# A weight product of 1160 columns, split 392, 384 and 384 instead of 512, 320 and 328

## The chip, the cores and the metric

The kernel runs on one core of a Trainium2 chip. The metric is the device time of one execution in microseconds. TensorE (PE) multiplies, VectorE (DVE), ScalarE (ACT) and GpSimd (POOL) work elementwise, SyncE (SP) issues most of the DMAs. A product takes a stationary operand of 128 x 128, loaded before it (PEld), and streams the columns of the moving operand through it into a PSUM bank of 512 float32 columns.

## The reference, cut to what matters

Two adapter layers over 4096 tokens (64 x 64) of width 1024:

```
x = x + A0[id] (B0[id] x)                     # low rank 16, one adapter of 64 for each sequence
base   = x W^T                                # 1024 x 1024
logits = x Wr^T + 5.0 * onehot(lang)          # 8 experts
gates  = softmax of the two largest logits
h      = x A^T                                # 8 experts x rank 16 = 128 columns
x = x + base + 2 * sum over e of gates_e (h_e B_e^T)
```

## The kernel before

The tokens are cut into T = 32 tiles of 128. Everything that the second layer multiplies x with stands in one matrix of 128 + 8 + 1024 = 1160 columns: A (ER = 128 columns), the router Wr (8 more, so NH = 136 columns ahead of W), and W transposed, with the identity added so that the product also gives x + base. It is kept in two halves, w_hi and w_lo, each with C = 8 chunks of 128 rows. A chunk takes PITCH = 1184 words, of which the last 24 are padding; the first chunk starts at word 28 of a line of 32.

Each tile needs x1_hi w_hi + x1_hi w_lo + x1_lo w_hi over 8 chunks, so K3 = 24 products for each group of columns. The 1160 columns are split into three PARTS, one for each of the PSUM banks O[0], O[1] and O[2]: columns 0 to 511, 512 to 831 and 832 to 1159. Part 0 holds h and the logits and 376 of the output's columns. make_part (line 602) issues the products of a part; first_part (578) does so for tile 0 in pieces between the transposes of the weight's nine blocks, and PART_BLOCKS says for which blocks each part waits.

TensorE's order for a tile n from 1 on (lines 689 to 705), written out by hand:

```
make_bx for 0 or 2 later tiles (line 501)
make_part(n, 0)              # 24 products; then the logits are there (h_psum)
add_l0(n + 1)  (n + 1 < 7)   # or
make_x1(n + 2) (n + 2 >= 7)  # lines 523 to 530; waits for bx_step, a_lo_ready, x_put
make_part(n, 1); turn_gated(n); make_part(n, 2) up to product 12
add_lora(0); add_lora(1)     # line 622, three products each, wait for gt_ready
make_part(n, 2) from product 12; add_lora(2)
```

From n = 5 on make_bx is done for two tiles together ahead of an odd n. Its result goes through ScalarE (swap and pair copies, lines 751 and 758) and VectorE (lines 965 to 980) to bx_t. VectorE then runs choose_experts and weigh_experts (998 to 1025), turns x1 of the next tile (924), makes the two halves of the turned gates (gated_t_part: gt_hi at 1031, gt_lo), x1_lo, and for later tiles b_raw (935), a_raw (945) and xt (917). a_raw goes to ScalarE for the high half of a_t (a_hi_part, 731) and to GpSimd for the low half (a_lo_part, 417), which tells a_lo_ready; between its a_lo_parts GpSimd gathers later adapters by indirect DMA. ScalarE copies the three banks to out_sb (out_part, 805), and SyncE stores a tile's row block when all three are there. The last tile is stored in three pieces (376, 320 and 328 columns).

add_lora streams lb_hi and lb_lo, whose 1024 columns start at word 4 of a line, so the slices for parts 1 and 2 (from columns 376 and 696) start at word 28.

Of the kernel before, what the change touches and what calls it, by code (L numbers as in the profile page):

```python
# [12 lines left out]
P = 128  # L13
LANG_BIAS = 5.0
BANK = 512
# [4 lines left out]
def two_adapter_layers(nc, x, adapter_ids, lang_ids, l0_A, l0_B, l1_W, l1_Wr, l1_A, l1_B, out):  # L20
    NB, S, D = x.shape
    NAD, R, _ = l0_B.shape
    E = l1_Wr.shape[0]
    T = NB * S // P
# [11 lines left out]
    PITCH = (NW + LINE - 1) // LINE * LINE  # L36
    REST = (NW - BANK) // 2 // LINE * LINE
    PARTS = [(0, BANK), (BANK, BANK + REST), (BANK + REST, NW)]
    NP = len(PARTS)
# [20 lines left out]
    with ExitStack() as ctx:  # L60
# [217 lines left out]
        UNIT_BANK_X0 = {12: 0, 13: 1}  # L278
        PART_BLOCKS = ((0, 1, 2, 3), (3, 4, 5, 6), (6, 7, 8))

# [8 lines left out]
        def weight_cols(b):  # L289
            return slice(0, ER) if b == 0 else slice(NH + (b - 1) * P, NH + b * P)  # L290

# [29 lines left out]
        def _(sp):  # L321
# [42 lines left out]
            for n in range(T):  # L364
# [6 lines left out]
                if n < T - 1:  # L371
                    for k in range(NP):
                        sp.wait_ge(out_ready[k], n + 1)
                    sp.dma_start(out_rows[n * P:(n + 1) * P, :], out_sb[:, n % 2, :]).then_inc(out_stored[n % 2], 16)
            for k, (lo, hi) in enumerate(PARTS):
                lo = max(lo - NH, 0)
                sp.wait_ge(out_ready[k], T)
                sp.dma_start(out_rows[(T - 1) * P:T * P, lo:hi - NH],
                             out_sb[:, (T - 1) % 2, lo:hi - NH]).then_inc(last_stored, 16)
            sp.wait_ge(out_stored[T % 2], 16 * (T // 2))  # L380
# [102 lines left out]
        def _(pe):  # L483
# [134 lines left out]
            def add_lora(part):  # L618
                lo, hi = PARTS[part]
                skip = NH if part == 0 else 0  # L620
                for k, (gt, lb) in enumerate(((gt_hi, lb_hi), (gt_hi, lb_lo), (gt_lo, lb_hi))):
                    mm = pe.matmul(O[part][:, skip:hi - lo], gt[:, :], lb[:, lo + skip - NH:hi - NH],  # L622
                                   start=False, stop=(k == 2), skip_group_check=True)
                mm.then_inc(o_psum, 1)
# [83 lines left out]
        def _(act):  # L708
# [90 lines left out]
            def out_part(n, part):  # L799
                lo, hi = PARTS[part]  # L800
                skip = NH if part == 0 else 0
                if part == 0 and n >= 2:
                    act.wait_ge(out_stored[n % 2], 16 * (n // 2))
                act.wait_ge(o_psum, NP * n + part + 1)
                nc.scalar.copy(out_sb[:, n % 2, lo + skip - NH:hi - NH],  # L805
                               O[part][:, skip:hi - lo]).then_inc(out_ready[part], 1)
# [402 lines left out]
```

## Time and profile before

| what | value |
|---|---|
| median of 3 runs | 525.18 us (523.86 to 525.43) |
| span of the profiled execution | 523.2 us |
| what lies around the span, by the median | 2.0 us |
| PE busy | 510.4 us, 98% |
| PEld / DVE / ACT / POOL busy | 89% / 73% / 46% / 33% |
| granted TensorE clock, mean | 0.993 |
| HBM traffic | 189 GB/s over the span |

The profiled execution is listed by its span, the time from the first to the last instruction; no time of its own is given beside it. A PE share of 98% doesn't say that TensorE is at its peak: neighbouring products overlap, and their ends are modelled.

### The profile page before, as it was taken

To read this page: it belongs to the slowest core of one execution; us is meant where nothing else is said; L and a number is where in the kernel's file an instruction comes from. 1 tells how busy PE (TensorE), PEld (TensorE's weight loads), DVE (VectorE), ACT (ScalarE), POOL (GpSimd) and SP (SyncE) were. 2 spreads that over 40 slices of the span, in tenths; PEclk is the share of its full clock that TensorE was granted. 3 is DMA by queue.
4 is the path that set the end of the run, shared out by engine and by line. 5 is a ranking of instruction groups with operands and counts; after the bars stand their busy time and mean duration, and the time that the engine had idled before them with its cause. 6 is when DMAs were issued, how large, how long until landed. Compare 5 with 4: busy or idle time off the path is not lost.

```text
span 523.2 us, 9432 instructions
## 1 busy us (share of the span) xinstructions
PE 510.4 (98%) x3350; PEld 465.7 (89%) x3350; DVE 383.9 (73%) x882; ACT 240.6 (46%) x543; POOL 171.1 (33%) x159
## 2 busy tenths in 40 slices
PE   7699999999899999999999999999999999999997
PEld 6588999889899899999989899998989999898997
DVE  5779686758879686977968697796969779693441
ACT  4655433545354544445454445554544545543221
POOL 5442325634314434142443414143441414321000
PEclk9799999999999999999999999999999999999999
DMA  8942455637757768477785857878576767633301
GB/s 330 322 114 82 130 134 170 205 111 233 231 185 231 229 153 260 169 219 238 245 239 152 248 184 222 247 222 245 155 225 207 243 225 213 202 105 98 122 40 41
DMA packets 52467, 99.76 MB, mean 191 GB/s; under 512 B 6716, under 2 KB 35260, under 8 KB 52420
## 3 DMA queue, kind: packets, MB, share of 16 engines
q1 hardware_dynamic: 45744, 78.14, 48.7%
q0 software_dynamic: 6656, 20.98, 12.7%
q8 instruction: 27, 0.44, 0.3%
q14 instruction: 20, 0.16, 0.1%
q10 hardware_dynamic: 20, 0.03, 0.0%
HBM read 69.24 MB, written 29.88 MB: 189 GB/s over the span
## 4 chain that ended last, share of the span: by engine, by line
PE 87%; DVE 7%; issue 2%; ACT 1%; DMA 1%; POOL 1%; another core or an unknown queue 0%; DVEq 0%; POOLq 0%
PE o_bank L609 69%; PE o_bank L622 8%; PE b_bank L501 2%; PE o_bank L598 2%; PE x_bank L529 2%; DMA a_in<-in_L_cond_A_dram,a_run 1%; DVE a_raw L945 1%; PE x_bank L519 1%; DVE x_lo L882 1%; PE b_bank L486 1%; DVE xt L917 1%; PE x_bank L486 1%; ACT bx_pair L758 1%; DVE w_in L924 0%; DVE b_raw L935 0%
## 5 line engine op out<-in xcount | busy, mean ns | idle before, releaser
L609 PE MATMUL o_bank<-w_hi,x_hi 128*128 128x512 f32 (+1 forms) x744 | 255.6, 344 | 0.0
L609 PE MATMUL o_bank<-w_lo,x_hi 128*128 128x512 f32 (+1 forms) x744 | 251.1, 337 | 0.0
L609 PE MATMUL o_bank<-w_hi,x_lo 128*128 128x512 f32 (+1 forms) x744 | 250.9, 337 | 0.0
L417 POOL TENSOR_TENSOR a_t<-a_raw,a_t 64x1024 fp32r<-64x1024 f32 x30 | 72.3, 2411 | 248.9 <-ACT a_t L731 178.3
L609 PEld LDWEIGHTS o_bank<-w_hi,x_hi 128*128 128x128 f32 x744 | 139.8, 188 | 13.5 <-issue 3.2
L609 PEld LDWEIGHTS o_bank<-w_lo,x_hi 128*128 128x128 f32 x744 | 139.9, 188 | 10.1
L609 PEld LDWEIGHTS o_bank<-w_hi,x_lo 128*128 128x128 f32 x744 | 139.7, 188 | 10.2
L945 DVE STREAM_TRANSPOSE a_raw<-a_in 128x1024 f32<-128x1024 f32 x32 | 65.3, 2044 | 2.8 <-DMA a_in<-in_L_cond_A_dram,a_run 2.8
L388 POOL DMA_INDIRECT a_in<-in_L_cond_A_dram,a_run x64 | 61.0, 952 | 19.3 <-issue 19.0
L731 ACT CAST a_t<-a_raw 128x1024 fp32r<-128x1024 f32 x32 | 33.6, 1050 | 70.0 <-DVE a_raw L945 69.9
L805 ACT COPY out_sb<-o_bank 128x376 f32<-128x376 f32 (+2 forms) x96 | 39.5, 443 | 52.6 <-PE o_bank L622 52.6
L924 DVE STREAM_TRANSPOSE w_in<-w_in 128x512 f32<-128x512 f32 x50 | 58.7, 1196 | 0.1
L917 DVE STREAM_TRANSPOSE xt<-x_in 128x512 f32<-128x512 f32 x50 | 56.1, 1158 | 0.0
L770 ACT CAST x_hi<-w_in 128x512 fp32r<-128x512 f32 x50 | 31.1, 621 | 43.2 <-DVE w_in L924 43.2
L758 ACT COPY bx_pair<-bx_half 32x128 f32<-32x128 f32 x120 | 35.6, 297 | 22.7 <-DVE bx_half L965 11.2
L394 POOL DMA_INDIRECT b_in<-in_L_cond_B_dram,b_run x32 | 30.8, 964 | 23.4 <-DVE a_t L882 8.6
L973 DVE TENSOR_TENSOR bx_all<-bx_half,bx_pair 128x128 f32<-128x128 f32 x30 | 8.8, 292 | 39.0 <-ACT bx_pair L758 37.6
L882 DVE TENSOR_TENSOR x_lo<-w_in,x_hi 128x512 fp32r<-128x512 f32 x50 | 35.0, 722 | 2.0 <-ACT x_hi L770 2.0
L622 PE MATMUL o_bank<-lb_hi,gt_hi 128*128 128x376 f32 (+2 forms) x96 | 30.6, 319 | 0.6 <-DVE gt_lo L882 0.6
L622 PE MATMUL o_bank<-lb_lo,gt_hi 128*128 128x376 f32 (+2 forms) x96 | 30.5, 318 | 0.0
L622 PE MATMUL o_bank<-lb_hi,gt_lo 128*128 128x376 f32 (+2 forms) x96 | 30.4, 317 | 0.0
L965 DVE TENSOR_TENSOR bx_half<-b_bank,bx_swap 128x128 f32<-128x128 f32 x30 | 8.6, 288 | 29.6 <-ACT bx_swap L751 27.7
(111 smaller groups left out, 504.3 us busy)
## 6 DMA issues: line engine op xcount, KB each, us to landing
out_dram<-out_sb SPq DMA_DIRECT2D x31, 512.0 KB
x_in<-in_x_dram SPq DMA_DIRECT2D x120, 128.0 KB
w_in<-in_x_dram SPq DMA_DIRECT2D x25, 512.0 KB
x_dram<-w_in SPq DMA_DIRECT2D x25, 512.0 KB, 4.4
w_in<-x_dram SPq DMA_DIRECT2D x100, 128.0 KB
w_in<-in_L_cond_W_dram SPq DMA_DIRECT2D x6, 512.0 KB, 13.3
x_in<-in_x_dram SPq DMA_DIRECT2D x2, 512.0 KB
out_sb<-in_L_cond_W_dram SPq DMA_DIRECT2D x2, 512.0 KB, 15.1
```

Of the source, the lines that this page charges most:

```text
L388: pool.indirect_dma_start(a_in[:, m % 2, b, :], None, l0_A_runs, bass.IndirectOffsetOnAxis(ap=a_run[:, m * BPT + b:m * BPT + b + 1], axis= ...
L417: nc.gpsimd.tensor_tensor(lower, a_raw[Q:P, m % 2, :], lower.bitcast(F32), ALU.subtract)\
L609: mm = pe.matmul(O[part][:, 0:hi - lo], xs[:, n % 2, c, :], w[:, c, lo:hi], start=(k == 0), stop=(k == K3 - 1), skip_group_check=True)
L622: mm = pe.matmul(O[part][:, skip:hi - lo], gt[:, :], lb[:, lo + skip - NH:hi - NH], start=False, stop=(k == 2), skip_group_check=True)
L731: nc.scalar.copy(a_t[:, m % 2, :], a_raw[:, m % 2, :]).then_inc(a_hi_ready, 1)
L758: nc.scalar.copy(bx_pair[q * SQ:(q + 1) * SQ, :], bx_half[o * SQ:(o + 1) * SQ, :]).then_inc(pair_ready, 1)
L770: nc.scalar.copy(x1_hi[:, m % 2, chunks(h), :], src).then_inc(x1_hi_ready, 1)
L805: nc.scalar.copy(out_sb[:, n % 2, lo + skip - NH:hi - NH], O[part][:, skip:hi - lo]).then_inc(out_ready[part], 1)
L882: return nc.vector.tensor_tensor(dst, raw, hi.bitcast(F32), ALU.subtract)
L917: nc.vector.transpose(xt[:, m % 2, chunks(h), :].rearrange("p k (g i) -> p k g i", i=SQ), src[:, chunks(h), :, :]).then_inc(t1_ready, 1)
L924: nc.vector.transpose(x1_t[:, chunks(h), :].rearrange("p k (g i) -> p k g i", i=SQ), src[:, chunks(h), :, :]).then_inc(x1t_ready, 1)
L945: nc.vector.transpose(cols, a_in[:, m % 2, :, :].rearrange("p b (f r) -> p f b r", r=R)).then_inc(aT_ready, 1)
```

## The change

The parts become columns 0 to 391, 392 to 775 and 776 to 1159 of the matrix, 392, 384 and 384 columns. The 24 words of padding move from the end of each chunk to between parts 0 and 1, so that part 1 starts at word 416 and part 2 at word 800 of a chunk, each again at word 28 of a line. The blocks of W that make up the parts become 0 to 2, 3 to 5 and 6 to 8, whole blocks each. The output's columns are split 256, 384 and 384 in place of 376, 320 and 328 (OUTS), in add_lora, in out_part and in the three stores of the last tile. The slices of lb_hi and lb_lo start at columns 0, 256 and 640, word 4 of a line each. The numbers of products, copies and DMAs stay as they were, and so does their order.

```
-    REST = (NW - BANK) // 2 // LINE * LINE
-    PARTS = [(0, BANK), (BANK, BANK + REST), (BANK + REST, NW)]
+    FIRST = 2 * P
+    HALF = (D - FIRST) // 2
+    GAP = PITCH - NW
+    PARTS = [(0, NH + FIRST), (NH + FIRST + GAP, PITCH - HALF), (PITCH - HALF, PITCH)]
+    OUTS = [(0, FIRST), (FIRST, FIRST + HALF), (FIRST + HALF, D)]
...
-        PART_BLOCKS = ((0, 1, 2, 3), (3, 4, 5, 6), (6, 7, 8))
+        PART_BLOCKS = ((0, 1, 2), (3, 4, 5), (6, 7, 8))
...
         def weight_cols(b):
-            return slice(0, ER) if b == 0 else slice(NH + (b - 1) * P, NH + b * P)
+            if b == 0:
+                return slice(0, ER)
+            at = NH + (b - 1) * P + (GAP if (b - 1) * P >= FIRST else 0)
+            return slice(at, at + P)
...
-            for k, (lo, hi) in enumerate(PARTS):
-                lo = max(lo - NH, 0)
+            for k, (lo, hi) in enumerate(OUTS):
...
-                    mm = pe.matmul(O[part][:, skip:hi - lo], gt[:, :], lb[:, lo + skip - NH:hi - NH],
+                    mm = pe.matmul(O[part][:, skip:hi - lo], gt[:, :], lb[:, OUTS[part][0]:OUTS[part][1]],
...
-                nc.scalar.copy(out_sb[:, n % 2, lo + skip - NH:hi - NH],
+                nc.scalar.copy(out_sb[:, n % 2, OUTS[part][0]:OUTS[part][1]],
```

## Rows read from the trace of the kernel before

**Rows 1.** The page: its span, TensorE's share, the chain that ended last.

```profile
span 523.2 us, 9432 instructions
...
PE 510.4 (98%) x3350; PEld 465.7 (89%) x3350; DVE 383.9 (73%) x882; ACT 240.6 (46%) x543; POOL 171.1 (33%) x159
...
PE 87%; DVE 7%; issue 2%; ACT 1%; DMA 1%; POOL 1%; another core or an unknown queue 0%; DVEq 0%; POOLq 0%
```

**Rows 2.** Chain in order of time, tiles 11 and 12: start us, us, what.

```profile
204.19 5.68 PE o_bank L609 x24
...
213.84 0.11 PE b_bank L486
...
218.96 5.50 PE o_bank L609 x24
...
224.92 3.51 PE o_bank L609 x24
...
228.54 1.81 PE o_bank L609 x12
...
231.31 1.81 PE o_bank L609 x12
...
234.58 0.42 PE o_bank L609
```

**Rows 3.** Timelines of tiles 11 and 12, by engine: start us, us, instruction.

```profile
204.25 0.54 ACT L751 COPY bx_swap<-b_bank 64x128 f32<-64x128 f32 x2 [0.61 <-PE b_bank L501]
...
210.56 0.15 DVE L998 SCALAR_TENSOR_TENSOR logit<-is_lang,o_bank 128x8 f32<-128x8 f32 x1
...
212.68 1.20 DVE L924 STREAM_TRANSPOSE w_in<-w_in 128x512 f32<-128x512 f32 x1
213.99 0.29 DVE L1031 CAST gt_hi<-b_bank 128x128 fp32r<-128x128 f32 x1
...
217.67 2.04 DVE L945 STREAM_TRANSPOSE a_raw<-a_in 128x1024 f32<-128x1024 f32 x1
...
219.75 1.05 ACT L731 CAST a_t<-a_raw 128x1024 fp32r<-128x1024 f32 x1 [2.58 <-DVE a_raw L945]
...
220.88 2.41 POOL L417 TENSOR_TENSOR a_t<-a_raw,a_t 64x1024 fp32r<-64x1024 f32 x1 [12.67 <-ACT a_t L731]
...
224.29 0.63 PE L529 MATMUL x_bank<-a_t,bx_t 128*128 128x512 f32 x2
```

**Rows 4.** Line 528, the wait of TensorE's sequencer in tile 12: ns, start us.

```profile
L528 PEldq EVENT_SEMAPHORE  x1: 3130/3130/3130, 220.2 to 220.2; - x1
```

**Rows 5.** Timeline, tile 10: first products of add_lora(0) and add_lora(1).

```profile
199.80 0.33 PE L622 MATMUL o_bank<-lb_hi,gt_hi 128*128 128x376 f32 x1
...
200.32 0.31 PE L622 MATMUL o_bank<-lb_hi,gt_hi 128*128 128x320 f32 x1
```

**Rows 6.** Timeline, tile 4: a product that waited for VectorE, and the next.

```profile
105.34 0.29 DVE L882 TENSOR_TENSOR gt_lo<-b_bank,gt_hi 128x128 fp32r<-128x128 f32 x1
...
105.69 0.44 PE L622 MATMUL o_bank<-lb_hi,gt_hi 128*128 128x376 f32 x1 [0.62 <-DVE gt_lo L882]
105.97 0.33 PE L622 MATMUL o_bank<-lb_lo,gt_hi 128*128 128x376 f32 x1
```

**Rows 7.** Timeline, tile 0: the first four products of part 0.

```profile
23.17 2.05 PE L598 MATMUL o_bank<-w_hi,x_hi 128*128 128x512 f32 x4
```

**Rows 8.** Timeline ahead of tile 7: VectorE, GpSimd and the wait of make_bx.

```profile
136.60 3.49 DVE L882 TENSOR_TENSOR x_lo<-w_in,x_hi 128x512 fp32r<-128x512 f32 x2
136.80 2.74 POOL L417 TENSOR_TENSOR a_t<-a_raw,a_t 64x1024 fp32r<-64x1024 f32 x1 [4.37 <-DMA a_in<-in_L_cond_A_dram,a_run]
...
142.74 0.64 PE L501 MATMUL b_bank<-xt,b_raw 128*32 128x128 f32 x16 [1.34 <-DVE b_raw L935]
```

**Rows 9.** Groups of ScalarE by form, 200 to 500 us: busy us, mean ns, idle before.

```profile
L805 ACT COPY out_sb<-o_bank 128x376 f32<-128x376 f32 x20 | 9.4, 472 | 13.3 <-PE o_bank L622 13.3
L805 ACT COPY out_sb<-o_bank 128x328 f32<-128x328 f32 x20 | 8.6, 428 | 20.1 <-PE o_bank L622 20.1
```

More of the change, by code:

```diff
@@ L374, in _ @@
                     sp.dma_start(out_rows[n * P:(n + 1) * P, :], out_sb[:, n % 2, :]).then_inc(out_stored[n % 2], 16)
-            for k, (lo, hi) in enumerate(PARTS):
-                lo = max(lo - NH, 0)
+            for k, (lo, hi) in enumerate(OUTS):
                 sp.wait_ge(out_ready[k], T)
-                sp.dma_start(out_rows[(T - 1) * P:T * P, lo:hi - NH],
-                             out_sb[:, (T - 1) % 2, lo:hi - NH]).then_inc(last_stored, 16)
+                sp.dma_start(out_rows[(T - 1) * P:T * P, lo:hi],
+                             out_sb[:, (T - 1) % 2, lo:hi]).then_inc(last_stored, 16)
             sp.wait_ge(out_stored[T % 2], 16 * (T // 2))
```

## The prediction

> **What bounds the kernel now.** I read the page first. TensorE is busy for 98% of the span and carries 87% of the chain that ended last, almost all of it in the weight product of line 609 [rows 1]. So TensorE sets the pace, and the question is what the new split does to its 2,232 products and to what it waits for. A matmul's own mean duration doesn't help here, since neighbours overlap; the chain in order of time gives the stretches without overlap [rows 2]. There, two token tiles (n = 11 and 12; tiles alternate like this to the end, a pair with two make_bx in front of its odd tile) take 234.58 - 204.19 = 30.39 us with no gap on TensorE. Then I looked for what reaches TensorE just in time, because a new split changes when each wait is reached: the timeline of the other engines over the same pair [rows 3] and the wait of TensorE's sequencer [rows 4].
>
> **The products themselves.** In the even tile part 0 (24 products of 512 columns) takes 5.50 us, 229.2 ns each; part 1 (24 of 320) 3.51 us, 146.3 ns each; part 2 (24 of 328) 1.81 + 1.81 = 3.62 us, 150.8 ns each [rows 2]. That is nearly a straight line: (229.2 - 146.3) / 192 = 0.432 ns a column, and 146.3 + 8 x 0.432 = 149.8 for 328. On that line 392 columns take 229.2 - 120 x 0.432 = 177.4 ns and 384 take 174.0 ns. Part 0 becomes 4.26 us, parts 1 and 2 4.18 us each, 12.61 us a tile against 12.63. Next to nothing is gained or lost: the number of products (72 a tile) and of columns (1160) is the same. The new parts still begin at word 28 of a 32-word line, since the 24 padding words stand after the column 392, so alignment of w_hi and w_lo gives no reason to leave the line.
>
> Bounds, since 384 and 392 columns don't occur in the trace: what a product takes beyond its columns at 2.4 GHz is 146.3 - 133.3 = 13.0 ns for 320 and 229.2 - 213.3 = 15.9 ns for 512. With 13.0 for all, three products take 522.2 ns, with 15.9 for all 530.9 ns, against 526.3 now. Over 24 x 31 = 744 such triples that is -3.1 us and +3.4 us if TensorE sets the pace everywhere. I take the line, because 328 lies within 1 ns of it.
>
> As a rule: the Trainium skill (TensorE: Matmul & The Clock Gate, section Back-to-back issue gap) gives N / 2.4 + 2.5 ns for a warm product. The trace disagrees in size: 229.2 ns for 512 columns where the rule has 215.8. The rule too is linear, so by it three products take 490.8 ns before and after, and part 0 gets shorter by 24 x 50.0 = 1.20 us where the rows give 1.24; the stall worked out below would be 0.16 us by it instead of 0.20.
>
> **The nine products of add_lora.** Three of 376 columns take 200.32 - 199.80 = 0.52 us, 173.3 ns each [rows 5]; on the line it would be 170.5, so they lie 3 ns above it. Its operand lb_hi starts at word 4 of a line, where parts 1 and 2 start at word 28 today; in the new split all three start at word 4. By the line, 3 x 118.6 + 6 x 174.0 = 1.40 us, as today (3 x (173.3 + 146.3 + 150.8) = 1.41 us); with 3 ns more on the six that move, 1.42 us. I take +0.02 us a tile; the bounds are 0 and 0.04.
>
> **What comes earlier, and the wait it reaches.** Part 0 is now 5.50 - 4.26 = 1.24 us shorter and parts 1 and 2 are 0.67 and 0.56 us longer. Everything that TensorE asks for behind part 0 is asked for 1.24 us earlier. That is the step that I expect to decide. In an even tile make_x1(n + 2) stands right behind part 0 and needs the lower half of a_t from GpSimd (a_lo_ready). The chain to it starts in the odd tile before, with make_bx on TensorE, and runs through ScalarE and VectorE: swap at 204.25 (the wait before it ended by TensorE), the bx chain, the gate, the turned x1, x_lo, a_raw at 217.67, a_t high half on ScalarE at 219.75, low half on GpSimd from 220.88 to 223.29 [rows 3]. TensorE reaches make_x1 at 224.29: 1.00 us to spare. The sequencer is there much sooner and stands in that wait from 220.2 for 3.13 us [rows 4], hidden now by products already queued.
>
> This chain doesn't get shorter with part 0. VectorE comes to choose_experts at 210.56, after two bx chains, when part 0 (204.19 + 5.68 = 209.87) is done already; from there to a_raw it works almost without a gap. One piece moves: gt_hi at 213.99 waits for the turned gates, since VectorE was free at 212.68 + 1.20 = 213.88 and starts a next instruction some 0.06 us before the end of the last. In the new split parts 0 and 1 of the odd tile together are 0.57 us shorter, the turned gates are there before, and gt_hi starts at 213.82. So the chain ends 0.17 us earlier, at 223.12.
>
> TensorE gets to make_x1 at 224.29 - 1.24 + 0.02 = 223.07. A late hand-over has a price of its own: where gt_lo ended at 105.63, the product behind it started at 105.69 and the next 0.28 us later instead of 0.17 [rows 6]; the first weight load is then not hidden. I take 0.05 + 0.10 us: make_x1 effectively at 223.27, a stall of **0.20 us**. The pair is then 30.59 us instead of 30.39. It can't be made up behind: from make_x1 to the next pair TensorE has its own work, and the next chain starts with its make_bx. The stall falls in the even tiles n = 8 to 28 (n + 2 up to 30), 11 times: 11 x 0.20 = **+2.2 us**. Bounds: no cost at the hand-over and the 0.17 gained, 0.05 us each, +0.6 us; nothing gained at gt_hi and the full hand-over, 0.37 us each, +4.1 us.
>
> The other waits behind part 0 hold: in the odd tile make_x1 needs only the first of the two bx chains, which are both done by about 210.6, so that the first is through well before 208.5; the gates are done when VectorE goes on to its next transpose at 212.68, and TensorE turns them at 213.84 - 0.57 = 213.3 [rows 2, 3]. What queues behind the stalled make_x1 is only TensorE's own part 1; ScalarE's copy of x1 and the logits of VectorE wait less than now.
>
> **First tiles.** Tile 0 runs its first four products of part 0 at the lower clock level: 2.05 us for four [rows 7], 0.43 us apart, which is 512 columns at 1.2 GHz. Fewer columns there save about 0.4 us, and it is given back, because parts 1 and 2 are longer and the chain of make_bx(2) is released as before. In tiles 1 to 6 TensorE already waits here and there on VectorE (1.3 us on b_raw in front of tile 7 [rows 8], 0.6 us on gt_lo in tile 4 [rows 6]); VectorE and ScalarE, which don't get faster, set the end of that stretch. A shift of TensorE alone is swallowed by the 1.3 us wait. I take 0, bounds -0.7 and +0.6 us. PART_BLOCKS asks for fewer blocks; those waits don't end late now, so nothing.
>
> **End.** The last copy has 384 columns instead of 328: by the copies' means (472 - 428) / 48 = 0.9 ns a column [rows 9], +0.05 us. The copies of parts 1 and 2 in the loop are longer and that of part 0 shorter; ScalarE idles there.
>
> **Sum.** 523.2 + 2.2 + 0.05, and 0 for the rest, is a span of about 525.4 us. The median of the runs is 525.18, 2.0 us above the span of the profiled execution (the span runs from the first instruction to the last). So 527.4 us.
>
> **Rivals.**
> (A) The forecast: GpSimd's a_lo decides the even tiles. 526.8 to 529.4 us. Chance 0.55.
> (B) The change does nothing: the line holds and the chain ends some 0.2 us earlier than I think, for instance because ScalarE's longer idle time lets a copy in before. All stalls are 0.05 or less: 525.2 + 0.5 = 525.7, between 524 and 526.5. For it: the margin that decides is 0.2 us of a 19 us chain. Chance 0.22.
> (C) Faster: the logits come 1.2 us earlier in each tile, and the 1.3 us wait on b_raw goes away. Two x_lo of VectorE shortly before it take 3.49 us, most of it beside GpSimd's a_t (136.80 to 139.54) [rows 8]. If both ended before 136.80, b_raw would come some 2 us sooner. The two take 1.3 us where GpSimd is idle, so they would have to start by 135.5, 1.1 us earlier; VectorE waits there for the turned gates and gains some 0.3 us. That is against it. With the 0.6 us of tile 4 too and no stall later: 525.2 - 1.3 - 0.6 = 523.3 us. Chance 0.12.
> (D) The products cost the upper bound: 530.9 - 526.3 = 4.6 ns a triple. TensorE's own pair is 30.39 + 48 x 0.0046 + 0.04 = 30.65 us, and since 0.16 us of that lies ahead of make_x1, the stall shrinks to 0.04: 30.69 us, 15 pairs, 525.2 + 4.5 = 529.7 us. Chance 0.11.
>
> **Numbers.** The likeliest is A, 527.4 (its own range 526.8 to 529.4). The range 524.3 to 530.0 takes in B nearly whole and D, and leaves out C and the tails. 0.3% is 1.6 us and about what a measurement tells from no change: slower by more than that, over 526.8, is A and D less the low edge of A, 0.60; within is most of B and a bit of A and C, 0.28; faster 0.12.
>
> **What the profile would show.** Products of 392 and 384 columns starting 177 and 174 ns after one another; part 0 at 4.26 us in the chain; in even tiles a gap of some 0.2 us on TensorE in front of line 529, released by GpSimd's a_t, and the chain in order of time going through GpSimd, ScalarE and VectorE 11 times; pairs of 30.6 us. The forecast is wrong if a pair takes 30.4 us with no gap (B), if make_bx in front of tile 7 starts 1 us earlier than at 142.74 (C), or if 384 columns take 176 ns (D).

## The result, and the profile after

The changed kernel takes **530.22 us** (median of 4 runs, 529.4 to 531.2) against 524.86 us (523.86 to 525.43) for the kernel before beside it: a ratio of 1.0107, 95% interval 1.0083 to 1.0131. The forecast was 527.4 us with a range up to 530.0. The sign was right, and about half of the loss was not foreseen.

The page of the changed kernel (its span, the busy shares, the chain that ended last), to be held against [rows 1]:

```profile
span 528.8 us, 9430 instructions
...
PE 516.1 (98%) x3350; PEld 498.9 (94%) x3350; DVE 380.4 (72%) x882; ACT 241.7 (46%) x543; POOL 171.2 (32%) x159
...
PE 88%; DVE 4%; issue 3%; ACT 1%; DMA 1%; another core or an unknown queue 1%; POOL 1%; DVEq 0%; POOLq 0%
```

The span grew by 5.6 us, and "another core or an unknown queue" now has 1% of the chain. There is one core only, so that entry is a wait whose releaser the profile doesn't show.

Next the chain of the changed kernel in order of time over tiles 11 and 12 (start us, us, what), the stretch of [rows 2]:

```profile
207.97 4.49 PE o_bank L614 x24
212.46 0.46 PE x_bank L534 x2
212.93 4.20 PE o_bank L614 x24
...
222.81 4.25 PE o_bank L614 x24
227.06 0.59 PE x_bank L534 x2
227.64 4.19 PE o_bank L614 x24
...
237.52 1.01 PE b_bank L506 x32
238.53 1.63 PE o_bank L614 x8
```

Part 0 takes 4.25 us (forecast 4.26) and part 1 4.19 (4.18). make_x1 (line 534 now) takes 0.59 us in the even tile and 0.46 in the odd one: there is the forecast stall, smaller than I made it. The pair, 207.97 to 238.53, is 30.56 us; over the ten pairs of tiles 8 to 27 the mean is 30.58 us against 30.39 before.

The waits of the changed kernel (engine, line, waited for: us in total, times, longest):

```profile
ACT bx_swap L756 <- remote: 3.7, 1, 3.7
PEld x_bank L534 <- DVE bx_t L985: 2.6, 1, 2.6
PEld x_bank L534 <- issue: 2.4, 11, 0.4
```

The third row, put down to "issue", is the stall of the ten even tiles from 10 to 28, and one wait more in tile 5; tile 8, behind the long tile 7, has no stall in this execution. The first two rows belong together and happen once, ahead of and in tile 7. As in the kernel before, make_bx for tiles 9 and 10 runs ahead of tile 7, and make_x1(9), for tile 9, stands in tile 7. The timeline of the changed kernel there (start, us, engine, line, what, in brackets the idle time before and its releaser):

```profile
141.86 0.96 POOL L399 DMA_INDIRECT b_in<-in_L_cond_B_dram,b_run  x1 [0.77 <-POOL a_t L422]
141.97 1.08 PE L506 MATMUL b_bank<-xt,b_raw 128*32 128x128 f32 x32
143.13 0.95 POOL L393 DMA_INDIRECT a_in<-in_L_cond_A_dram,a_run  x1 [0.30 <-issue]
144.38 0.95 POOL L393 DMA_INDIRECT a_in<-in_L_cond_A_dram,a_run  x1 [0.30 <-issue]
146.21 0.54 ACT L756 COPY bx_swap<-b_bank 64x128 f32<-64x128 f32 x2 [3.66 <-remote]
149.79 1.22 PE L534 MATMUL x_bank<-a_t,bx_t 128*128 128x512 f32 x2 [2.25 <-DVE bx_t L985]
```

make_bx ended at 141.97 + 1.08 = 143.05, and ScalarE, which waits for both of its results, began the swap at 146.21: 3.16 us late. TensorE then stood 2.25 us in front of make_x1(9). Two stretches of the changed kernel, around that stand and over a steady pair (us, then busy us of PE, PEld, DVE, ACT and POOL with their instructions, granted clock, DMA share, GB/s):

```profile
141.00:156.30 15.30, 13.05 (x92) 12.06 (x91) 5.90 (x25) 6.54 (x19) 2.95 (x4) 0.89 0.72 215
208.00:238.50 30.50, 30.50 (x201) 29.64 (x201) 23.84 (x54) 14.86 (x34) 9.01 (x8) 1.00 0.67 202
```

From 149.5 us, in the last 0.3 us of that stand, to 152.9 us the granted clock was 0.5 (1.2 GHz), and the part 1 that fell into it took 5.12 us in the chain instead of 4.20. Tile 7 took 18.68 us from its part 0 to the next, against 14.70 before.

So the 5.6 us are: **+4.0 us** in tile 7, **+2.0 us** from tile 8 to the end, and -0.3 us from the start to tile 7. Of these only the second was forecast.

### The profile page after: what moved, and what is told of

Same layout as the page of the kernel before. It is cut to its first block, busy times and chain, and to the rows that moved or that the text cites. A ratio compares the mean times of both kernels' runs of the same rounds, so it can differ in the third digit from the quotient of the medians.

```text
span 528.8 us, 9430 instructions
## 1 busy us (share of the span) xinstructions
PE 516.1 (98%) x3350; PEld 498.9 (94%) x3350; DVE 380.4 (72%) x882; ACT 241.7 (46%) x543; POOL 171.2 (32%) x159
## 4 chain that ended last, share of the span: by engine, by line
PE 88%; DVE 4%; issue 3%; ACT 1%; DMA 1%; another core or an unknown queue 1%; POOL 1%; DVEq 0%; POOLq 0%
PE o_bank L614 69%; PE o_bank L627 8%; PE o_bank L603 3%; PE x_bank L534 3%; PE b_bank L506 2%; DMA a_in<-in_L_cond_A_dram,a_run 1%; PE x_bank L524 1%; PE x_bank L491 1%; ACT bx_pair L763 1%; DVE a_raw L950 1%; PE b_bank L491 1%; PE o_bank L491 0%; DVE b_raw L940 0%; ACT bx_swap L756 0%
## 5 line engine op out<-in xcount | busy, mean ns | idle before, releaser
L614 PE MATMUL o_bank<-w_hi,x_hi 128*128 128x392 f32 (+1 forms) x744 | 256.6, 345 | 0.0
L614 PE MATMUL o_bank<-w_lo,x_hi 128*128 128x392 f32 (+1 forms) x744 | 252.1, 339 | 0.0
L614 PE MATMUL o_bank<-w_hi,x_lo 128*128 128x392 f32 (+1 forms) x744 | 251.7, 338 | 0.0
L810 ACT COPY out_sb<-o_bank 128x384 f32<-128x384 f32 (+1 forms) x96 | 41.9, 443 | 63.2 <-PE o_bank L627 61.3
L887 DVE TENSOR_TENSOR x_lo<-w_in,x_hi 128x512 fp32r<-128x512 f32 x50 | 32.8, 678 | 2.0 <-ACT x_hi L775 2.0
L627 PE MATMUL o_bank<-lb_hi,gt_hi 128*128 128x384 f32 (+1 forms) x96 | 30.6, 319 | 0.2 <-DVE gt_lo L887 0.2
L627 PE MATMUL o_bank<-lb_hi,gt_lo 128*128 128x384 f32 (+1 forms) x96 | 30.5, 318 | 0.0
L627 PE MATMUL o_bank<-lb_lo,gt_hi 128*128 128x384 f32 (+1 forms) x96 | 30.2, 315 | 0.0
```

What stands on the lines that cost most here:

```text
L614: mm = pe.matmul(O[part][:, 0:hi - lo], xs[:, n % 2, c, :], w[:, c, lo:hi], start=(k == 0), stop=(k == K3 - 1), skip_group_check=True)
L627: mm = pe.matmul(O[part][:, skip:hi - lo], gt[:, :], lb[:, OUTS[part][0]:OUTS[part][1]], start=False, stop=(k == 2), skip_group_check=True)
L810: nc.scalar.copy(out_sb[:, n % 2, OUTS[part][0]:OUTS[part][1]], O[part][:, skip:hi - lo]).then_inc(out_ready[part], 1)
L887: return nc.vector.tensor_tensor(dst, raw, hi.bitcast(F32), ALU.subtract)
```

## The experiments

They ran in five sets, each on one chip and with its own runs of the kernel before; sets 3 and 5 had the same chip, the others one each. Tile 7 is measured from the first product of its part 0 to that of tile 8, and a pair is the mean of the ten pairs of tiles 8 to 27. "Late" is the time from the end of make_bx(10) to the start on ScalarE of what waits for it, in front of tile 7; where all is well it is 0.07 us. The ratio is not that of the two medians: the kernel before had up to 35 runs in a set, and the two ways of comparing differ by up to 0.3%.

```
set  kernel         median us  ratio  95% interval      tile 7   late   pair
 1   before         523.00
     again          524.91     1.0031 1.0013 to 1.0049  14.75    0.07   30.58
     x1_later       523.52     1.0004 0.9984 to 1.0023  14.75    0.07   30.44
     split_448      522.56     1.0000 0.9979 to 1.0021  14.73    0.07   30.47
     no_gap         522.66     0.9990 0.9973 to 1.0008  14.67    0.07   30.44
 2   before         524.33
     before_again   524.41     0.9993 0.9980 to 1.0007  15.53    1.70   30.39
     again2         529.55     1.0096 1.0071 to 1.0121  17.53    3.11   30.60
     no_gap_x1      525.95     1.0027 1.0012 to 1.0042  17.05    2.68   30.37
     before_x1      526.11     1.0025 1.0011 to 1.0039  15.49    1.67   30.39
 3   before         522.48
     again3         525.16     1.0038 1.0019 to 1.0056  14.75    0.07   30.59
     odd_12         525.11     1.0028 1.0008 to 1.0049  14.73    0.07   30.59
     no_gap_12_6    521.73     0.9967 0.9948 to 0.9985  14.66    0.07   30.34
     split_448b     523.17     0.9994 0.9976 to 1.0012  14.72    0.07   30.47
 4   before         524.11
     before_late    526.00     1.0023 1.0007 to 1.0040  15.44    1.62*  30.39
     after_late     531.51     1.0129 1.0106 to 1.0153  20.01    4.60*  30.61
     odd_12_late    535.13     1.0223 1.0170 to 1.0276  20.58    4.61*  30.89
     x1_12_6_late   531.30     1.0104 1.0066 to 1.0141  20.56    4.63*  30.62
```

(* with the 1.54 us that these kernels add. The pair of before_x1 is that of its tiles without a late result. The pairs of odd_12_late and x1_12_6_late hold a second late result in tile 9; without tiles 8 and 9 they are 30.62 and 30.34.)

**The changed kernel again, set 1 (again).** No edit.

> The changed kernel once more, unaltered. Its first profile shows three sources of the 5.6 us: pairs of tiles of 30.56 us instead of 30.39 (about +2.0 us), and one event in tile 7 in which ScalarE's bx_swap starts 3.2 us after make_bx ended, and TensorE then waits 2.3 us and runs some products at 1.2 GHz. Theory E (the event belongs to the kernel): it is there again at the same place, the time is 529 to 531 us and the span 527 to 529. Theory F (the event was an accident of one execution): it is gone, and the span is about 525.5 us; but then the other runs of the kernel, all over 529 us, would want another reason.

Measured: 1.0031, pairs of 30.58 us, and a tile 7 of 14.75 us. The forecast part of the loss is there, the rest isn't, and no profile of this set shows the event. That is theory F's sign, but the four runs of the first measurement, all over 529 us, still spoke against an accident. The timeline of this run at the same place:

```profile
139.39 0.96 POOL L399 DMA_INDIRECT b_in<-in_L_cond_B_dram,b_run  x1 [0.95 <-DVE b_raw L940]
139.51 1.08 PE L506 MATMUL b_bank<-xt,b_raw 128*32 128x128 f32 x32
140.65 0.95 POOL L393 DMA_INDIRECT a_in<-in_L_cond_A_dram,a_run  x1 [0.30 <-issue]
140.66 0.54 ACT L756 COPY bx_swap<-b_bank 64x128 f32<-64x128 f32 x2 [0.56 <-PE b_bank L506]
```

The same order of work, but here the swap follows make_bx by 0.07 us. This execution also shows what holds make_x1 in the even tiles, which the name "issue" hides. GpSimd's a_lo_part and make_x1's first weight load in tile 12:

```profile
218.15 2.42 POOL L422 TENSOR_TENSOR a_t<-a_raw,a_t 64x1024 fp32r<-64x1024 f32 x1 [12.63 <-ACT a_t L736]
...
220.65 0.30 PEld L534 LDWEIGHTS x_bank<-a_t,bx_t 128*128 128x128 f32 x2 [0.16 <-issue]
```

GpSimd ends at 218.15 + 2.42 = 220.57 and the load starts 0.07 us later (before rounding), as it does in all 11 even tiles from 8 to 28. In the kernel before, the load starts 0.78 us after GpSimd's end (224.07 against 223.29), in split_448 below mostly 0.50 us.

**make_x1 six products later (x1_later).** The stall alone is taken away:

```
+                make_part(n, 1, 0, 6)
                 if K <= n + 2 < T:
                     make_x1(n + 2)
-                make_part(n, 1, 0, K3)
+                make_part(n, 1, 6, K3)
```

> The changed kernel with make_x1(n + 2) moved behind the sixth product of part 1, 1.04 us later on TensorE. Theory A (GpSimd's lower half of a_t holds TensorE up in 11 even tiles): the gap and the late start of line 534 are gone, pairs of tiles take 30.4 us, some 2 us less over the kernel. Theory D (the products of 384 and 392 columns are what costs): pairs stay at 30.56 us and the time stays. The event of tile 7 is no part of either; make_x1(9) comes 1 us later there, so up to 1 us of that wait may be covered too.

The chain of this kernel in tile 12 and the start of 13:

```profile
216.88 5.29 PE o_bank L614 x30
222.17 0.46 PE x_bank L534 x2
222.63 3.15 PE o_bank L614 x18
...
231.47 1.01 PE b_bank L506 x32
```

make_x1 is back at 0.46 us in the even tile and the pair is 30.44 us (expected 30.4). So the stall was worth 30.58 - 30.44 = 0.14 us a pair, and 0.05 us of the 0.19 that a pair lost is left for the products and add_lora. By medians the whole loss of set 1 (1.91 us) shrinks to 0.52 us.

**Part 0 halfway (split_448).** The kernel before with parts of 448, 352 and 360 columns:

```
-    PARTS = [(0, BANK), (BANK, BANK + REST), (BANK + REST, NW)]
+    PARTS = [(0, 448), (448, 800), (800, NW)]
```

> The kernel before with parts of 448, 352 and 360 columns, padding at the end as before, all parts starting at word 28. Part 0 is then 24 x 64 x 0.432 ns = 0.66 us shorter than with 512 columns, and 0.34 us of the 1.00 us to spare are left. Theory A: no stall, pairs of 30.4 us, in the pairs no loss. Theory D (a product costs more beyond its columns when the three are more alike): about half of the loss, pairs of 30.47 us. Theory E for the event of tile 7 says nothing certain: if it depends on TensorE reaching make_bx in front of tile 7 without a wait, it may be there or not, and the time is 525 or 528 us.

No stall (make_x1 as in odd tiles) and 1.0000: part 0 may lose 0.6 us, but not 1.24, before GpSimd's a_lo decides. The pair is 30.47 us all the same, 0.08 us above the kernel before, and that is the figure that I had given theory D. Its three products together take 526.8 ns against 525.5 in the kernel before, an estimate of 0.06 us a pair. So theory D is there too, but small: it can't be the 0.14 us that went with x1_later.

**The padding back at the end (no_gap).** Same split, parts 1 and 2 at word 4 of a line:

```
-    GAP = PITCH - NW
-    PARTS = [(0, NH + FIRST), (NH + FIRST + GAP, PITCH - HALF), (PITCH - HALF, PITCH)]
+    GAP = 0
+    PARTS = [(0, NH + FIRST), (NH + FIRST, NW - HALF), (NW - HALF, NW)]
```

> The changed kernel with the 24 words of padding back at the end of each chunk, so that parts 1 and 2 (384 columns each) start at word 4 of a line instead of word 28. The products of add_lora that start at word 4 were 3 ns above the line at 376 columns. If that is the place of the start in the line, 48 products in each of 31 tiles cost 3 ns each more, +4.5 us where TensorE sets the pace, less what the stall of theory A gives back: 532 to 534 us. If the start doesn't matter: as the changed kernel, 530 us.

The opposite came: 522.66 us, 2.25 us less than the changed kernel beside it. From start to start a product of 384 columns takes 172.1 ns here and 174.6 ns at word 28; one of 392, at word 28 in both, 179.6 against 177.9 ns. Three products together are 523.8 against 527.2 ns (525.5 in the kernel before), 3.4 x 744 = 2.5 us. A part of that is given back in add_lora, whose products of 384 columns take 175.4 ns here and 171.0 in the changed kernel. In the pairs the padding costs 30.58 - 30.44 = 0.14 us, and 0.07 us in the two kernels without a stall (x1_later and no_gap_x1 below). Putting it between the parts did cost time. That the start in the line is the reason is not shown: the products of 392 columns and those of add_lora changed too, and their operands start where they did.

**Both kernels on the second chip (before_again, again2).** No edit.

> The kernel before, unaltered, for a profile beside those of the changed kernel on the same chip. If the late releases that neither profile explains (VectorE's gt_hi 1.1 us late in tile 4 of the kernel before, ScalarE's bx_swap 3.7 us late in tile 7 of the changed kernel, both from one and the same chip) belong to the chip or the moment, this profile has none, tile 4 takes 16.3 us instead of 17.1 and the span is about 0.8 us shorter than the first, for the same start. If they belong to the kernel, tile 4 takes 17.1 us again. The wait on b_raw in front of tile 7 should be there in either case (tile 6 17.2 us).

> The changed kernel a third time. Theory F (the event of tile 7 was an accident): ratio to the kernel before 1.003, as in the second measurement, and no late bx_swap. Theory E: 1.010 again and the event in tile 7.

The first measurement is back: 1.0096, and tile 7 at 17.53 us, so the event goes with the chip and isn't an accident of one execution. In the kernel before tile 4 takes 17.02 us, as in its first profile. The kernel before has a late result too, in a weaker form. Its timeline in front of tile 7, and the turned gates behind it:

```profile
141.20 1.08 PE L501 MATMUL b_bank<-xt,b_raw 128*32 128x128 f32 x32
141.90 0.96 POOL L394 DMA_INDIRECT b_in<-in_L_cond_B_dram,b_run  x1 [1.29 <-DVE b_raw L935]
...
143.98 0.55 ACT L751 COPY bx_swap<-b_bank 64x128 f32<-64x128 f32 x2 [2.24 <-remote]
...
152.55 0.33 PE L486 MATMUL b_bank<-ident,gated 128*128 128x128 f32 x1 [0.61 <-DVE gated L1025]
```

143.98 - 142.28 = 1.70 us late, and tile 7 loses 15.53 - 14.69 = 0.84 us. The 1.3 us wait on b_raw of [rows 8], which I expected in either case, is 0.2 us in this execution; tile 6 takes 15.69 us and not 17.25.

The chain of the changed kernel in the same set shows what the late result has to get through:

```profile
148.00 0.35 DVE bx_t L985
148.35 0.21 DVE bx_half L970
...
151.13 0.17 DVE logit L1003
...
153.05 0.30 DVE gated L1030
153.35 0.04 issue
153.40 0.33 PE b_bank L491
```

It doesn't leave VectorE at bx_t, although make_x1(9) waited for that (2.20 us). It goes on through the second bx chain, the experts and the gates to turn_gated, 8.58 us from the swap at 144.82. TensorE comes there after parts 0 and 1, which are 0.57 us shorter in the changed kernel. Slack is the lateness that costs nothing, so it is lateness less loss: 1.70 - 0.84 = 0.86 us in the kernel before, 3.11 - 2.78 = 0.33 us in the changed one. (The 0.07 us of a swap that is on time is counted in both; the delay that costs nothing is that much smaller.) The difference, 0.53 us, is about that of parts 0 and 1. It explains the smaller part of 2.78 - 0.84 = 1.94 us. The other 1.41 us are the greater lateness itself, 3.11 against 1.70.

**Both repairs, and a control (no_gap_x1, before_x1).** no_gap with make_x1 six products later, and the kernel before with make_x1 six products later.

> The changed kernel with both edits: padding at the end of each chunk (products of 384 columns start at word 4 and take 172.1 ns instead of 174.6), and make_x1 behind six products of part 1 (no stall). If the two are separate causes they add: a pair takes 30.44 - 0.13 = 30.31 us, and with the b_raw wait gone as in the changed kernel the time is some 3 us below the changed kernel and 1 to 2 us below the kernel before. If the stall hides what the products gain, it is the same as with one of them, 30.44 us a pair.

> Control: the kernel before with make_x1 behind six products of part 1. There TensorE had 1.00 us to spare at make_x1, so theory A has nothing to win: pairs of 30.39 us and a ratio of 1.000. If pairs get shorter here too, moving make_x1 saves something else than the wait for a_t, and the gain in the changed kernel says nothing on theory A.

no_gap_x1: pairs of 30.37 us, but tile 7 lost 17.05 - 14.66 = 2.39 us at a lateness of 2.68; slack 0.29 us, as in again2. The later make_x1 gave no cover, and instead of the expected gain of 1 to 2 us the kernel lost against the kernel before (1.0027). before_x1: its pairs without a late result are 30.39 us, as expected of the control, so moving make_x1 saves nothing of itself. The ratio is 1.0025 and not 1.000, because tiles 7, 11, 15 and 21 have a result 1.7 us late, each costing 0.80 to 0.83 us, and tile 25 one that is 1.0 us late and costs 0.12 us: the slack of 0.86 us again. The place of make_x1 doesn't matter for a late result; turn_gated does.

**Later in odd tiles, and the three together (again3, odd_12, no_gap_12_6, split_448b).** The edit of the middle two; the third also has the padding at the end and 6 for 0:

```
+                cut = 12 if n % 2 else 0
+                make_part(n, 1, 0, cut)
                 if K <= n + 2 < T:
                     make_x1(n + 2)
-                make_part(n, 1, 0, K3)
+                make_part(n, 1, cut, K3)
```

> The changed kernel unaltered, to have its profile beside the next three. Where make_bx's result reaches ScalarE 2 us or more late in front of tile 7, tile 7 takes 17 to 19 us and the ratio to the kernel before is about 1.010; where it does not, tile 7 takes 14.75 us and the ratio is 1.003. Pairs from tile 9 on take 30.58 to 30.60 us in both.

> The changed kernel with make_x1 behind 12 products of part 1 in the odd tiles only, so that 4.26 + 2.10 = 6.4 us of TensorE's own work lie between make_bx and the product that needs bx_t (4.3 us in the changed kernel, 5.5 us before). Theory 1 (the late result costs time because part 0 is too short to cover it): with the late result there, tile 7 takes 15.0 us or less instead of 17 to 19, and the kernel is 2.5 us or more faster than the changed kernel beside it; the pairs stay at 30.58, since the stall of the even tiles is untouched. Theory 2 (the time is lost to something else at that place, such as the clock or the weight loads, and the late result is only its sign): tile 7 stays above 16.5 us. If no late result shows, nothing changes, within 0.5 us, and the run tells nothing about it.

> The changed kernel with its padding at the end of each chunk, and make_x1 behind 12 products of part 1 in odd tiles and behind 6 in even tiles. If the causes named so far are all there is (the stall of the even tiles, the uncovered late result, 2.5 ns for each product of 384 columns that starts at word 28), it takes 1 to 2.5 us less than the kernel before: pairs 30.3 us or less, tile 7 15 us or less. If moving make_x1 itself brings late results in other tiles, as in the kernel before with make_x1 moved, it stays within 1 us of the kernel before or above it.

> The kernel before with parts of 448, 352 and 360 columns: part 0 takes 4.9 us, halfway between the two kernels. Theory 1: with the late result there, tile 7 loses about half of what it loses in the changed kernel, some 1.5 to 2 us against 0.8 in the kernel before, and the ratio is about 1.002. Theory 2: what tile 7 loses does not go with the length of part 0. Without a late result the ratio is 1.000 as it was beside the first four.

No result was late in this set, so odd_12 and split_448b tell nothing on that. again3 repeats again (1.0038). no_gap_12_6 is the best version found: 521.73 us, 0.9967 of the kernel before (by the medians 0.75 us less, which is what 0.05 us in each of 15 pairs makes), with the chain of a pair free of stalls (tile 12 and the make_bx behind it):

```profile
215.35 5.34 PE o_bank L614 x30
220.69 0.46 PE x_bank L534 x2
221.16 3.11 PE o_bank L614 x18
...
229.93 1.01 PE b_bank L506 x32
```

**A delay put in by hand (before_late, after_late, odd_12_late, x1_12_6_late).** Four kernels (before, changed, odd_12, no_gap_12_6) with twelve extra copies on ScalarE in front of the swap:

```
                 act.wait_ge(bx_psum, made)
...
+                if m == 9:
+                    act.wait_ge(ident_set, 1)
+                    for k in range(12):
+                        nc.scalar.copy(spare[:, k, :], ident[:, 0:LINE])
```

> The kernel before with twelve copies of 32 columns on ScalarE, into words that nobody reads, in front of the swap for tile 9, the place where the late result was seen. They delay that swap by d, some 2.4 us. TensorE reaches make_x1(9) with 1.9 us to spare and make_x1(10), a tile later, with 1.0 us (the chain to it runs through the same swap), so tiles 7 and 8 together lose d - 1.0 = 1.4 us. If a late swap is not what cost the time in the changed kernel, this run only says what ScalarE's delay costs.

> The changed kernel with the same delay d. To spare are 0.6 us at make_x1(9) and nothing at make_x1(10), so tile 7 loses d - 0.6 = 1.8 us and tiles 7 and 8 together all of d, 2.4 us: 1 us more than the kernel before loses. Theory 1 (length of part 0): that difference, and a tile 7 of 16.5 us as where the result was late by itself. Theory 2 (something else at this place costs the time): tile 7 loses less than 1 us.

> The changed kernel with make_x1 behind 12 products of part 1 in odd tiles, and the same delay d. At make_x1(9) there are now 2.7 us to spare, so tile 7 loses nothing (14.75 us), but make_x1(10) in tile 8 still has none, so that tile 8 loses all of d, 18.2 us instead of 15.8. If instead tiles 7 and 8 together lose less than 1 us, VectorE makes up for the delay on the way, and part 0 in front of make_x1(9) was the only thing that mattered.

> The version with padding at the end and make_x1 behind 12 products of part 1 in odd and 6 in even tiles, and the same delay d. 2.7 us are to spare at make_x1(9) and about 0.9 at make_x1(10): tile 7 14.7 us, tile 8 d - 0.9 = 1.5 us longer than 15.7. The loss is then that of the kernel before, and the slack at make_x1(10) is what a version has to have.

The copies took 1.54 us, not 2.4. before_late: the swap began 1.62 us after make_bx's end and tile 7 lost 15.44 - 14.69 = 0.75 us, tile 8 nothing: a slack of 0.87 us. So a late swap alone does what before_again shows. In the other three the result was late by itself too, by 3.06 to 3.09 us, so they have 4.6 us and don't measure the delay d alone. odd_12_late in front of and in tile 7:

```profile
145.69 1.54 ACT L762 COPY spare<-ident 128x32 f32<-128x32 f32 x12 [3.56 <-remote]
147.23 0.54 ACT L764 COPY bx_swap<-b_bank 64x128 f32<-64x128 f32 x2
...
150.82 0.73 PE L535 MATMUL x_bank<-a_t,bx_t 128*128 128x512 f32 x2 [1.62 <-DVE bx_t L993]
...
155.81 0.33 PE L492 MATMUL b_bank<-ident,gated 128*128 128x128 f32 x1 [2.17 <-DVE gated L1038]
```

TensorE stands less in front of make_x1(9), 1.62 us against 3.70 in after_late, and stands again, 2.17 us, in front of the turned gates. Tile 7 is 20.58 us, no shorter than after_late's 20.01. My expectations for tile 7 (16.5, 14.75 and 14.7 us) were wrong in all three: I had counted the slack at make_x1(9) and at make_x1(10) and passed over turn_gated between them. In all three the granted clock fell to 0.5 for 3.4 us at the end of a stand or just behind it, which adds to the loss: 20.01 - 14.75 = 5.26 us in after_late for 4.60 us of lateness.

In odd_12_late and x1_12_6_late tile 9 had a late result as well, without added copies and with the clock at 1.0. That is the test that odd_12 missed. Tile 9 lost 17.53 - 14.73 = 2.80 us at a lateness of 3.11, and 17.48 - 14.66 = 2.82 us at 3.12: the slack of 0.3 us of the changed kernel, although make_x1 stands 12 products later. Theory 1 of odd_12, that a short part 0 in front of make_x1 is the reason, is wrong; the slack that decides is that of turn_gated.

**What makes the result late (gather_later, all_three).** I counted TensorE's semaphore increments by whether their instruction ends in the 1.25 us behind the start of one of GpSimd's gathers, and whether the increment is recorded within 0.1 us, later, or not within 4 us (missing):

```
                              in a gather             outside
kernel (set)           on time  late  missing   on time  late  missing
before (first)            35     21     16        209      3      3
after (first)             34     10     22        210      9      2
before_again (2)          40     19     12        211      5      0
again2 (2)                41     13     13        213      5      2
after_late (4)            33     13     22        212      4      3
again (1)                 64      0      3        220      0      0
again3 (3)                61      0      5        221      0      0
```

On some chips about half of the increments that fall into a gather are late or missing, on others nearly none. Where make_bx's were late, the b_in gather had begun before make_bx ended: 0.4 us before it in before_again (1.70 us late), 0.8 us in no_gap_x1 (2.68 us late), 1.2 us in again2 and in the first profile of the changed kernel (3.1 us late). In the first profile of the kernel before, the wait on b_raw held make_bx(10) back until it ended 0.07 us ahead of the gather, and nothing was late; before_late is the same.

The steady tiles are a test of this within each run, since make_bx and the gathers fall differently there. From tile 7 on, the ten profiles of the first measurement and of sets 2 and 4 have 120 pairs of make_bx. In 14 a gather had begun 0.3 to 1.2 us before the second one ended, and all 14 results were late, by 1.0 to 3.2 us. In one it had begun 0.02 us before, in 105 none had in the 1.25 us before: all 106 were on time. In sets 1 and 3 a gather had begun 0.1 to 1.2 us before the end 11 times, and none was late. So on some chips a result was late when, and only when, a gather had been under way for 0.3 us or more as make_bx ended.

The traces also tie the event to the change. In front of tile 7 the b_in gather waits for the b_raw that frees its buffer, and it starts 0.77 or 0.78 us behind that b_raw's end, in before and before_again as in after and again2. In the two profiles of the kernel before TensorE is there first, and make_bx starts within 0.1 us of b_raw's end. Its end then comes 0.4 us behind the gather's start in before_again, and 0.07 us ahead of it in before, where make_bx(9) had run already. In the changed kernel b_raw is done 0.9 us before TensorE comes to make_bx, and the gather starts 1.2 us ahead of make_bx's end.

gather_later was to part the two by a wait on GpSimd:

```
                 pool.wait_ge(a_lo_ready, m + 1)
+                if m % 2 == 0 and m > K and m + 2 < T:
+                    pool.wait_ge(bx_psum, m + 3)
                 for b in b_loads(m):
```

> The changed kernel with one more wait on GpSimd: from tile 7 on, in odd tiles, its three gathers start only when both make_bx have told their result. On the chips where the result is late, TensorE's signals that fall into a gather are late or missing in the records (in the changed kernel with the delayed swap 35 of 68, against 7 of 219 outside), on the others 0 to 5 of some 65. Theory 1 (gathers hold up the signal of make_bx): on a chip of the first kind, told by its share of late signals in the first 140 us, make_bx's signals in front of tile 7 come 0.04 us after the products, tile 7 takes 14.75 us instead of 17.5 to 20, and the ratio is that of the stall alone, 1.003 to 1.005 instead of 1.010. Theory 2 (the gathers only happen to be there): tile 7 stays at 17.5 us or more. On a chip of the second kind the ratio is 1.003 and nothing is told.

> The same wait on GpSimd in the version with padding at the end and make_x1 behind 12 products of part 1 in odd and 6 in even tiles. It takes away all three causes named: tile 7 14.7 us, pairs 30.34 us, and on a chip of either kind 1.5 to 2.5 us less than the kernel before, ratio 0.995 to 0.998. Without the cause from the gathers being right it stays within 0.3% of the kernel before on a chip of the first kind (1.000 to 1.003, as the version with make_x1 6 products later there).

They took 634.10 us (1.2107, 1.2078 to 1.2136) and 605.11 us (1.1540, 1.1516 to 1.1563), because I put the wait one a_lo_part too early: the gathers that meet make_bx stand behind a_lo_part(9), so m should be odd. The waits of gather_later:

```profile
POOL b_in L399 <- issue: 149.6, 16, 14.5
PEld x_bank L536 <- issue: 85.9, 11, 8.7
```

The wait held the gathers of the tile ahead back by up to 14.5 us, the adapters landed late, and TensorE stood up to 8.7 us in front of make_x1. Nor was any result late on that chip (gathers of gather_later: 68 on time, 1 late). This is the chip of set 3, where none had been late before either. So both say nothing about the cause. Whether a late signal becomes punctual when its gathers are held behind it, on a chip that has late ones, was not tried, and stays open.

## Why the prediction was right or wrong

**The products: nearly right.** 177.9 ns for 392 columns and 174.9 and 174.4 for 384, against 177.4 and 174.0 on the line; three together 527.2 ns against 525.5 measured the same way before. That is 1.7 ns a triple and 0.08 us a pair, for which I had nothing. Rival D's 4.6 ns a triple fell. What I didn't see is that the line holds for this layout only: with the padding at the end 384 columns take 2.5 ns less and 392 take 1.7 more (no_gap).

**add_lora: right to 0.03 us.** Six and three products take 0.87 + 0.52 = 1.39 us a tile in the chain of after, against 1.40 before (0.95 + 0.45); I had +0.02, it is -0.01. The 3 ns "above the line" at word 4 were no penalty of the word: in the changed kernel add_lora's 384 columns from word 4 take 171.0 ns, 3 ns below the line.

**The stall at make_x1: right mechanism, mis-sized.** It is there in the even tiles from 8 to 28, where and as forecast (in the first profile not in tile 8), released by GpSimd's a_lo, and goes with x1_later. It is 0.14 us, not 0.20, so 11 x 0.14 = 1.5 us for 2.2. The mis-sized term is mostly how much sooner the chain ends. From the start of the odd tile's part 0 to GpSimd's end it takes 19.17 us in the kernel before and 18.94 in most pairs of the changed one, 0.23 us less where I had 0.17. That the pairs give +2.0 us for the forecast +2.2 is partly luck: the 0.08 us of the products, which I had at nothing, made up for the smaller stall. Where no result is late, the ratio is 1.0031 and 1.0038, which on 525.18 us is 526.8 and 527.2 us. Rival B fell.

**First tiles: the failed step.** "A shift of TensorE alone is swallowed by the 1.3 us wait. I take 0." Up to tile 7 the sum came out (-0.3 us), but by luck and not as I said: terms of +0.75 and -1.5 us and smaller ones between happened to cancel. In tile 1 add_l0(2) has a stall of its own, up to 0.8 us at its first weight load, and the tile is 16.98 us instead of 16.23. The wait on b_raw went away, so that make_bx started at 141.97 and not 142.74, nearly the sign that I had named for rival C, and tile 6 gained 1.5 us. But that wait isn't a fixed property of the kernel before: before_late has it again, before_again has 0.2 us of it. And I had not asked what else it did: in the first profile it kept make_bx's signal ahead of GpSimd's gathers. The earlier b_raw, which rival C counted as a gain, goes with a gather that starts ahead of make_bx's end. What the prediction had at 0 there was in truth a result 3.16 us late in front of tile 7, and with it +4.0 us in that tile.

**"The other waits behind part 0 hold": the second half of the failed step.** They hold in the steady pairs, where nothing stands at turn_gated. But I only gave the two times (gates done at 212.68, TensorE there at 213.3) and didn't ask how late a result this margin of 0.6 us would bear. The late results size it: 0.86 us to spare at turn_gated in odd tiles before, 0.3 us after. Against a result 3.1 us late that leaves 2.8 us (again2); in the first measurement the clock at 0.5 behind the stand comes on top, 4.0 us in all.

**What is shown and what isn't.** That lateness costs its size less the slack, as long as the clock stays up, is shown: by before_late with a delay of known size, by the four kernels of set 2, and by tile 9 of two kernels of set 4. The slack comes out at 0.9 us for the kernel before and 0.3 us for the changed one each time. That on some chips make_bx's result is late when a gather is under way as it ends is shown by 14 cases with and 105 without. That the gather holds the signal up is the likeliest reading, but no run held the gathers back on such a chip. Nor is it shown why one chip has it and another not.

## What to carry to other kernels

When a change makes a stretch of one engine shorter, list every wait behind it with its slack in us, those that "hold" too, since the small slacks decide on the day when something upstream is late. A wait seen in one execution may be absent in the next, so don't rest a term on it without a second profile; and run the comparison on more than one chip where half a per cent matters. A reordering that hides one late hand-over is worth nothing if the next one on the same chain has less to spare.

## What the runs showed of the hardware

- make_bx's semaphore increments came up to 3.1 us after the products' end by the records, where one of GpSimd's indirect gathers (0.95 us each, 1.25 us apart) was under way, on the chips of sets 2 and 4 and in the first measurement. On those of sets 1 and 3 they came 0.04 us after the end, gather or not. The trace calls the wait "remote".
- A product of 384 columns of the weight takes 172.1 ns with the padding at the end (start at word 4 of a line of 32) and 174.6 ns with it between the parts (word 28). In the same two kernels the products of add_lora with 384 columns, which start at word 4 in both, take 175.4 and 171.0 ns. The Trainium skill (TensorE: Matmul & The Clock Gate, section Back-to-back issue gap) gives N / 2.4 + 2.5 for the isolated gap of one product, by estimate 162.5 ns; none of these rows agrees.
- Where TensorE stood for 2.3 us (after) or 3.7 us (after_late) in front of make_x1(9), the granted clock fell to 0.5 in the last 0.3 to 0.6 us of the stand and stayed there for 3.4 us; with a stand of 2.2 us in again2 it stayed at 1.0.
